# Expert tiles of a decoder kernel: the first product computed transposed, with copied weight chunks as the stationary operand and biases as one value per partition

## Chip, cores and metric

One Trainium2 chip, one of its cores. The metric is the device time of one execution in microseconds; lower is better. A program of this size is one launch with no work on the host.

## The reference

Six pre-norm residual layers act on x of shape 4 × 512 × 128: causal attention with 16 heads (A0), cross attention on 77 context rows (X0), a mixture of experts (M0), attention (A1), single-head cross attention (X1) and a quantized convolutional feed-forward layer (F1). The change lies in M0:

```
logits = xn @ gate_w + gate_b            # 8 experts
weights, indices = top_k(logits, 2); weights = softmax(weights)
h = xn @ w1[e] + b1[e]                   # 128 -> 1024
xh, gh = split(h, 2)                     # "plain" and "gated" half, 512 each
out_e = (silu(gh) * xh) @ w2[e] + b2[e]  # 512 -> 128
x = x + sum over the two chosen experts of weight * out_e
```

## The kernel before

All five engines run long hand-ordered queues. The first stream is A0 and X0 in 32 units (one unit: four heads of one batch), then M0, then a second stream with A1, X1 and F1.

**Loads.** SyncE (SP) issues nearly all DMAs from one queue, in an order written by hand. In unit `g` of the first stream it issues `load_sp` for unit `g + 3` (the stacked queries and keys of four heads go into a slot of `stk`, two DMAs of 256 KB), then `shift_sp` for unit `g + 1` (a small DMA from `negT` into `stk`, L625, one per unit), then two entries of the list `later` (weights and biases of later layers), then one 512 KB piece of the expert weights `w12`. Among the entries of `later` is `b1_gated`, the gated half of M0's first bias, spread over 128 partitions: 2048 KB. The plain half, `b1_plain`, lies in the bytes of `stk` and is loaded by `moe_sp` once X0's scores are done, 2048 KB too. TensorE's `max_pe` of unit `g + 2` runs beside the scores of unit `g` and waits for its slot of `stk`.

**M0.** Every token goes to two experts. GpSimd scatters the normed rows into expert regions of a DRAM tensor, 128 rows a tile; 39 tiles (`BUSY_TILES`) are then worked one after the other, each with the expert number read from a coded register (`codes`, `experts`). Per tile:

- SP loads 128 rows into `x_in` (two buffers), TensorE transposes them (`turn`, L1753), VectorE copies them to `x_inT` and computes the row numbers `y_at` (`turned`, L1637, L1638).
- `hidden` (L1759): for z = 1 (gated) and z = 0 (plain) one fp32 product, `x_inT` stationary, 512 columns of `w1` moving. It appears as two matmul instructions, as does every fp32 product here. The results have tokens on the partitions.
- VectorE adds `b1_gated` (L1644), ScalarE computes Silu (L1802), VectorE adds `b1_plain` (L1651) and multiplies (L1655) into `act`.
- TensorE transposes `act` in four chunks (`turn_act`, L1767), ScalarE copies the result to `actT` (L1806), TensorE computes the second product, four chunks of `actT` stationary, 128 columns of `w2` moving (`output`, L1774: eight instructions), VectorE adds `b2` (L1661), GpSimd stores the rows by an indirect DMA (L1742).

`x_inT`, `silu`, `y_sb` and the two banks for the hidden product (`hid`) are double; `act`, `actT` and `y_bank` are single. TensorE's order for tile t of the loop is: gated product of t + 1, transposes of `act` of t, turn of t + 2, plain product of t + 1, output of t. In the trace `probs` is the memory of `silu`, `y_sb`, `x_in` and `x_inT`; `oT` is `act`, `okT` is `actT`, `w` is the memory of the expert weights.

Of the kernel before, what the change touches and what calls it, by code (L numbers as in the profile page):

```python
# [11 lines left out]
F32 = mybir.dt.float32  # L12
# [239 lines left out]
def build(nc, d, out):  # L252
# [4 lines left out]
    with es:  # L257
# [71 lines left out]
        b1_gated = sb("b1_gated", [P, NE, FF])  # L329
        b1_plain = stk[:].rearrange("p u z h n -> p (u z h n)").bitcast(F32).rearrange("p (e n) -> p e n", e=NE)  # L330
# [1152 lines left out]
        def second_stream_sp(e):  # L1483
# [13 lines left out]
            diff expo plus recip gates zeroed scattered xT xT_out gated_half gated plain_half plain silu act actT actT_out y_in y_out  # L1497
# [86 lines left out]
        def moe_dve(e, ln):  # L1584
# [56 lines left out]
            def gated(t, ex):  # L1641
                k = t % 2
                e.wait_ge(m["gated_half"], t + 1)
                e.tensor_tensor(silu[:, k], hid[k][1], b1_gated[:, bass.ds(ex[t], 1)].rearrange("p o n -> p (o n)"), ALU.add)\  # L1644
                    .then_inc(m["gated"], 1)

            def product(t, ex):
                k = t % 2
                e.wait_ge(m["plain_half"], t + 1)
                wait(e, m["act"], t)  # L1650
                e.tensor_tensor(act[:], hid[k][0], b1_plain[:, bass.ds(ex[t], 1)].rearrange("p o n -> p (o n)"), ALU.add)\  # L1651
                    .then_inc(m["plain"], 1)
# [11 lines left out]
            e.wait_ge(s_biases, 16 * 2)  # L1664
            e.wait_ge(m["tile_e"], CODED + 2)
            code = codes(e)
            ex = experts(code, 0)
            for t in range(2):
                turned(t)
            gated(0, ex)  # L1670
            product(0, ex)
            for t in range(BUSY_TILES):
                if t + 1 < BUSY_TILES:
                    if t + 1 not in ex:
                        ex |= experts(code, t + 1)
                    gated(t + 1, ex)
                if t + 2 < BUSY_TILES:
                    turned(t + 2)
                if t + 1 < BUSY_TILES:
                    product(t + 1, ex)  # L1680
                output(t, ex)
# [24 lines left out]
        act = oT[:, 0]  # L1706
        actT = okT
# [7 lines left out]
        t_bank = bank_st[3]  # L1715
# [29 lines left out]
        def moe_pe(e, ln):  # L1745
# [9 lines left out]
            def hidden(t, ex, z):  # L1755
                if z == 1:
                    e.wait_ge(m["xT_out"], t + 1)
                    wait(e, m["act"], t - 1)
                e.matmul(hid[t % 2][z], x_inT[:, t % 2],  # L1759
                         w1[:, bass.ds(ex[t], 1), z * FF:(z + 1) * FF].rearrange("p o n -> p (o n)"),  # L1760
                         start=True, stop=True).then_inc(m["gated_half" if z else "plain_half"], 1)

            def turn_act(t):
                e.wait_ge(m["act"], t + 1)
                wait(e, m["actT_out"], t)
                for c in range(FC):
                    mm = e.transpose(t_bank[:, c * P:(c + 1) * P], act[:, c * P:(c + 1) * P], ident[:])  # L1767
                mm.then_inc(m["actT"], 1)

            def output(t, ex):  # L1770
                e.wait_ge(m["actT_out"], t + 1)
                e.wait_ge(m["y_out"], FREE + t)
                for c in range(FC):
                    mm = e.matmul(y_bank[:, 0:D], actT[:, c * P:(c + 1) * P],  # L1774
                                  w2[:, bass.ds(ex[t], 1), c, :].rearrange("p o n -> p (o n)"), start=(c == 0), stop=(c == FC - 1))
# [5 lines left out]
            ex = experts(code, 0)  # L1781
            for z in (1, 0):
                hidden(0, ex, z)
            for t in range(BUSY_TILES):
                if t + 1 < BUSY_TILES:
                    if t + 1 not in ex:
                        ex |= experts(code, t + 1)
                    hidden(t + 1, ex, 1)
                turn_act(t)
                if t + 2 < BUSY_TILES:  # L1790
                    turn(t + 2)
                if t + 1 < BUSY_TILES:
                    hidden(t + 1, ex, 0)
                output(t, ex)

        def moe_act(e, ln):
# [3 lines left out]
            def gate_part(t):  # L1800
                e.wait_ge(m["gated"], t + 1)
                e.activation(silu[:, t % 2], silu[:, t % 2], ACT.Silu).then_inc(m["silu"], 1)  # L1802

            def turned_act(t):
                e.wait_ge(m["actT"], t + 1)
                e.copy(actT[:], t_bank).then_inc(m["actT_out"], 1)  # L1806

            gate_part(0)
            for t in range(BUSY_TILES):
                turned_act(t)  # L1810
                if t + 1 < BUSY_TILES:
                    gate_part(t + 1)
# [150 lines left out]
        def weights_pe(e):  # L1963
            e.wait_ge(f["abs"], 2)
# [274 lines left out]
        halves = d["M0_b1"].rearrange("o (e z n) -> o e z n", e=NE, z=2)  # L2239
        later += [(b1_gated[:], halves[:, :, 1].to_broadcast([P, NE, FF]))]  # L2240
# [148 lines left out]
```

## Time and profile before

| what | value |
|---|---|
| three runs | 845.04, 848.81, 851.72 us; median 848.81 us |
| span of the profiled execution | 844.2 us |
| TensorE busy, share of the span | 689.9 us, 82% |
| VectorE busy | 589.3 us, 70% |
| ScalarE busy | 414.1 us, 49% |
| GpSimd busy | 285.0 us, 34% |
| mean granted TensorE clock | 0.880 of full |

The profiled execution has no time of its own beside its span; the fastest timed run lies 0.8 us above that span and the median 4.6 us above it. A busy share is a mean over stages with different limits, so what the change is worth is read stage by stage.

### The profile page before, as it was taken

Reading aid. Unit: us, or ns where it says so; the run is one execution under the profiler, and the core shown is the slowest. Engines: PE = TensorE matmul, PEld = TensorE weight load, DVE = VectorE, ACT = ScalarE, POOL = GpSimd, SP = SyncE. Lnnn points to the kernel's source line nnn. Section 1 sums busy time; section 2 is a strip of 40 time slices with the busy share of each in tenths; the row PEclk is TensorE's granted clock in tenths of the full one; section 3 lists DMA queues with packets and bytes.
Section 4 is the critical chain, followed back from the end, with each engine's and each line's share of the span. In section 5 each row is a group of like instructions: output and inputs, shape, how many; then the busy total and the mean of one; then the engine's idle time right before and its main releaser. Section 6 shows DMA issues by size and latency. Waiting matters only on the chain.

```text
span 844.2 us, 14947 instructions
## 1 busy us (share of the span) xinstructions
PE 689.9 (82%) x4693; PEld 333.1 (39%) x4698; DVE 589.3 (70%) x1606; ACT 414.1 (49%) x708; POOL 285.0 (34%) x504
## 2 busy tenths in 40 slices
PE   2759999989888998239999973668899988999887
PEld 1334454444434445116666641212232322324443
DVE  3757678686646664738788753778889898962664
ACT  1332556555665443003333322137688787885454
POOL 4742454543532233723222320122423133230310
PEclk9875999998988657569999995559999999999998
DMA  7443665482232314311111113521122210000000
GB/s 217 150 176 107 190 183 155 125 262 78 83 93 53 94 47 128 96 36 38 43 41 45 39 29 105 169 75 52 63 90 89 64 52 26 26 2 1 0 26 26
DMA packets 74780, 71.27 MB, mean 84 GB/s; under 512 B 14560, under 2 KB 67168, under 8 KB 74704
## 3 DMA queue, kind: packets, MB, share of 16 engines
q1 hardware_dynamic: 72000, 64.84, 25.1%
q0 software_dynamic: 2272, 4.69, 1.8%
q8 instruction: 40, 0.66, 0.3%
q10 hardware_dynamic: 432, 0.79, 0.3%
q14 instruction: 36, 0.29, 0.1%
HBM read 41.90 MB, written 28.00 MB: 83 GB/s over the span
## 4 chain that ended last, share of the span: by engine, by line
PE 62%; DVE 18%; issue 7%; POOL 4%; DMA 4%; ACT 4%; SPq 1%; DVEq 0%; POOLq 0%; ACTq 0%
PE bank_pv L732 11%; DVE mx L590 9%; PE bank_turn L574 8%; PE bank_scores L2024 5%; PE bank_scores L684 4%; PE bank_scores L1774 4%; PE bank_turn L1759 4%; PE bank_scores L1759 4%; PE bank_turn L751 3%; POOL routed_tokens L1726 2%; PE bank_scores L1767 2%; PE bank_turn L793 2%; PE bank_turn L528 2%; DMA stk<-stack_A 1%; DVE stats L450 1%
## 5 line engine op out<-in xcount | busy, mean ns | idle before, releaser
L590 DVE TENSOR_REDUCE mx<-bank_turn 128x1 f32<-128x512 f32 (+3 forms) x452 | 260.6, 616 | 67.2 <-PE bank_turn L579 35.8
L574 PE MATMUL bank_turn<-stk 64*128 64x77 bf16 (+4 forms) x708 | 164.2, 314 | 29.4 <-DVE mx L590 17.7
L684 PE MATMUL bank_scores<-stk 64*128 64x512 bf16 (+4 forms) x576 | 176.4, 372 | 4.8 <-ACT probs L705 3.6
L709 ACT ACTIVATE probs<-bank_scores 128x1024 f32<-128x1024 f32 (+4 forms) x160 | 117.2, 768 | 111.7 <-PE bank_scores L684 111.4
L705 ACT ACTIVATE probs<-bank_scores 128x512 f32<-128x512 f32 x256 | 138.6, 605 | 35.3 <-PE bank_scores L684 34.3
L732 PE MATMUL bank_pv<-probs,vsl 128*32 128x512 f32 (+4 forms) x1152 | 143.0, 570 | 2.8 <-POOL probs L717 1.9
L574 PEld LDWEIGHTS bank_turn<-stk 64*128 64x128 bf16 x708 | 54.4, 102 | 134.5 <-DVE mx L590 63.2
L717 POOL TENSOR_SCALAR_AFFINE_SELECT probs<-probs 128x256 f32<-128x256 f32 x128 | 52.1, 410 | 78.1 <-ACT probs L709 76.8
L1742 POOL DMA_INDIRECT expert_outputs<-probs,y_at x39 | 37.4, 960 | 101.0 <-DVE probs L1661 98.0
L477 POOL TENSOR_TENSOR rstd<-var,mhalf 128x4 f32<-128x4 f32 x24 | 25.4, 1058 | 119.2 <-DVE var L456 119.1
L1806 ACT COPY okT<-bank_scores 128x512 f32<-128x512 f32 x39 | 22.9, 587 | 80.8 <-PE bank_scores L1767 80.8
L528 PE MATMUL bank_turn<-ident,xn 128*128 128x128 f32 x60 | 13.2, 358 | 57.0 <-DVE xn L471 57.0
L684 PEld LDWEIGHTS bank_scores<-stk 64*128 64x128 bf16 (+1 forms) x576 | 47.6, 97 | 30.0 <-ACT probs L705 18.0
L579 PE MATMUL bank_turn<-behind_even,even_q 64*128 64x128 bf16 x256 | 53.4, 230 | 0.0
L578 PE MATMUL bank_turn<-behind_pair,pair_q 64*128 64x128 bf16 x256 | 53.4, 230 | 0.0
L1774 PEld LDWEIGHTS bank_scores<-w,okT 128*128 128x128 f32 x312 | 37.7, 191 | 25.0 <-issue 25.0
L2024 PE MATMUL bank_scores<-f_w1c,w 128*128 128x512 f32 x96 | 46.0, 616 | 0.4 <-ACT w L537 0.4
L1774 PE MATMUL bank_scores<-w,okT 128*128 x312 | 43.9, 284 | 0.8 <-ACT okT L1806 0.8
L604 POOL CAST neg<-mx 128x16 bf16<-128x16 f32 x33 | 6.5, 198 | 111.5 <-DVE mx L590 98.1
L590 DVE TENSOR_REDUCE mx<-bank_scores 128x1 f32<-128x512 f32 x60 | 40.8, 680 | 3.0 <-PE bank_scores L574 2.9
L1759 PE MATMUL bank_turn<-w,probs 128*128 x80 | 42.5, 616 | 0.0
L542 ACT COPY xnT<-bank_turn 128x512 f32<-128x512 f32 x19 | 11.1, 584 | 56.9 <-PE bank_turn L528 56.9
(299 smaller groups left out, 1179.7 us busy)
## 6 DMA issues: line engine op xcount, KB each, us to landing
stk<-stack_A SPq DMA_DIRECT2D x64, 256.0 KB, 3.2
w<-in_M_w SPq DMA_DIRECT2D x12, 512.0 KB, 4.7
stack_A<-parts SPq DMA_DIRECT2D x15, 384.0 KB, 3.1
stack_A<-fill SPq DMA_DIRECT2D x8, 512.0 KB, 5.1
stk<-stack_X SPq DMA_DIRECT2D x16, 256.0 KB, 2.7
stack_A<-parts SPq DMA_DIRECT2D x15, 256.0 KB, 3.2
probs<-routed_tokens SPq DMA_DIRECT2D x39, 65.0 KB, 1.8
b_gated<-in_M_b SPq DMA_DIRECT2D x1, 2048.0 KB, 11.9
```

What stands on the lines that cost most here:

```text
L574: mm = e.matmul(o, stk[r, slot, 0, pp, qt * P:(qt + 1) * P], stk[r, slot, 1, pp, 0:keys], start=True, stop=not a.causal)
L578: e.matmul(o, half(pair_q, j), half(behind_pair, j), start=False, stop=False)
L579: mm = e.matmul(o, half(even_q, j), half(behind_even, j), start=False, stop=True)
L590: e.tensor_reduce(o.rearrange("p h q -> p q h"), bank_of((g, m))[:, 0:k * keys].rearrange("p (q h k) -> p q h k", q=len(tiles), h=len(hs)) ...
L684: mm = e.matmul(score_bank(g, kt, i)[0:a.kp, 0:S - q0], stk[r, slot, 1, pp, kt * P:kt * P + a.kp], stk[r, slot, 0, pp, q0:S], start=True, ...
L705: e.activation(probs[:, probs_of(g, kt), j + 2 * pp], score_bank(g, kt, i), ACT.Exp, scale=1 / math.sqrt(HD)).then_inc(s["probs"], 1)
L709: e.activation(probs[0:a.kp, probs_of(g, kt), j:HG:2, 0:n], bank_scores[0:a.kp, 2 * j:2 * j + 2, 0:n], ACT.Exp, scale=1 / math.sqrt(HD)).t ...
L717: e.affine_select(out=o, in_=o, compare_op=ALU.is_ge, fill=0.0, base=0, pattern=[[0, 2], [1, P]], channel_multiplier=-1).then_inc(s["maske ...
L732: mm = e.matmul(bank_pv[VW * h:VW * (h + 1), q0:S], vsl[0:a.kp, slot, kt, h, :], probs[0:a.kp, probs_of(g, kt), h, 0:S - q0], start=(kt == ...
L1759: e.matmul(hid[t % 2][z], x_inT[:, t % 2], w1[:, bass.ds(ex[t], 1), z * FF:(z + 1) * FF].rearrange("p o n -> p (o n)"), start=True, stop=T ...
L1774: mm = e.matmul(y_bank[:, 0:D], actT[:, c * P:(c + 1) * P], w2[:, bass.ds(ex[t], 1), c, :].rearrange("p o n -> p (o n)"), start=(c == 0), ...
L2024: e.matmul(bank, f_xT[:, b, j * P + tap:j * P + tap + P], f_w1c[:, tap], start=(tap == 0), stop=False)
```

## The change

The first product of each expert tile is computed transposed: chunks of 128 columns of `w1` are the stationary operand and `x_inT` (128 tokens) moves, so that the result has hidden features on the partitions and tokens along the free axis. It then needs no transpose ahead of the second product: `turn_act`, `turned_act`, `actT` and `t_bank` go away. A bias is now one value per partition: Silu takes it as ScalarE's bias operand, the plain half takes it in one VectorE instruction that adds it and multiplies by Silu's result. The 1024 biases of the eight experts are loaded as 64 rows of 128 values (`b1_rows`, 32 KB), transposed once on TensorE and copied to `b1_cols` by VectorE; `b1_gated` and `b1_plain` and their two DMAs of 2048 KB go away. VectorE's and ScalarE's elementwise work on the hidden layer is now four instructions of 128 × 128 each, with the expert's column read through a register.

```
-        b1_gated = sb("b1_gated", [P, NE, FF])
-        b1_plain = stk[:]... (a view)
+        b1_rows, b1_cols = sb("b1_rows", [NE * 2 * FC, P]), sb("b1_cols", [P, NE, 2 * FC])
+        w_now = sb("w_now", [P, 2, 2 * FF])
...
 # VectorE
-            def gated(t, ex): ...
             def product(t, ex):
                 k = t % 2
                 e.wait_ge(m["plain_half"], t + 1)
-                wait(e, m["act"], t)
-                e.tensor_tensor(act[:], hid[k][0], b1_plain[...ex[t]...], ALU.add).then_inc(m["plain"], 1)
-                e.wait_ge(m["plain"], t + 1)
-                e.wait_ge(m["silu"], t + 1)
-                e.tensor_tensor(act[:], act[:], silu[:, k], ALU.mult).then_inc(m["act"], 1)
+                for c in range(FC):
+                    e.wait_ge(m["silu"], FC * t + c + 1)
+                    e.scalar_tensor_tensor(act[:, k, c * P:(c + 1) * P], hid[k][0][:, c * P:(c + 1) * P],
+                                           b1_cols[:, bass.ds(ex[t], 1), c], silu[:, k, c * P:(c + 1) * P],
+                                           ALU.add, ALU.mult).then_inc(m["act"], 1)
+            def weight(t, ex):
+                e.tensor_copy(w_now[:, t % 2, 0:FF], w1[:, bass.ds(ex[t], 1), 0:FF]...).then_inc(m["plain_w"], 1)
 # prologue: weight(0), weight(1), turned(0), turned(1), product(0), weight(2)
 # loop for t: turned(t + 2), product(t + 1), weight(t + 3), output(t)
...
 # TensorE
+                e.wait_ge(m["gated_w" if z else "plain_w"], t + 1)
                 for c in range(FC):
-                e.matmul(hid[t % 2][z], x_inT[:, t % 2], w1[...512 columns...], start=True, stop=True)
+                    o = z * FF + c * P
+                    mm = e.matmul(hid[t % 2][z][:, c * P:(c + 1) * P], w_now[:, t % 2, o:o + P], x_inT[:, t % 2],
+                                  start=True, stop=True)
-            def turn_act(t): ...
 # loop for t: hidden(t + 1, 1), turn(t + 2), hidden(t + 1, 0), output(t)
...
 # ScalarE, loop for t
+                e.wait_ge(m["gated_half"], t + 1)
+                for c in range(FC):
+                    e.activation(silu[:, t % 2, c * P:(c + 1) * P], hid[t % 2][1][:, c * P:(c + 1) * P], ACT.Silu,
+                                 bias=b1_cols[:, bass.ds(ex[t], 1), FC + c]).then_inc(m["silu"], 1)
+                    weight(t + 2)      # e.copy of the gated half into w_now, after the four
-            turned_act(t), gate_part(t + 1)
...
 # SyncE
-            e.dma_start(b1_plain, halves[:, :, 0].to_broadcast([P, NE, FF])).then_inc(s_biases, 16)
-        later += [(b1_gated[:], halves[:, :, 1].to_broadcast([P, NE, FF]))]
+        later += [(b1_rows[:], d["M0_b1"].rearrange("o (r p) -> (o r) p", p=P))]
...
 # ahead of the loop, in weights_pe and weights_dve
+            e.transpose(b1_bank, b1_rows[:], ident[0:NE * 2 * FC, 0:NE * 2 * FC]).then_inc(m["b1_in"], 1)
+            e.wait_ge(m["b1_in"], 1)
+            e.tensor_copy(b1_cols[:].rearrange("p e c -> p (e c)"), b1_bank).then_inc(m["b1"], 1)
```

## Rows read from the trace of the kernel before

**Rows 1.** Windows: start:end, length, busy us (count) per engine, clock, DMA share, GB/s.

```profile
173.00:186.00 13.00, 11.88 (x143) 5.91 (x140) 11.87 (x36) 7.63 (x13) 5.95 (x15) 1.00 0.95 293
186.00:188.00 2.00, 0.00 (x0) 0.00 (x0) 1.47 (x3) 0.00 (x0) 1.96 (x4) 1.00 1.07 391
190.00:197.00 7.00, 7.00 (x43) 3.16 (x44) 2.75 (x7) 4.13 (x6) 1.64 (x4) 0.54 0.44 154
...
381.00:500.00 119.00, 118.33 (x622) 72.81 (x620) 95.37 (x220) 42.83 (x74) 35.52 (x37) 1.00 0.15 41
```

**Rows 2.** Chain that ended last, one expert tile: start, us, what.

```profile
430.51 0.96 PE bank_scores L1774 x8
431.47 0.86 PE bank_turn L1759 x2
432.33 0.44 PE bank_scores L1767 x4
432.77 0.11 PE bank_turn L1753
...
433.74 0.96 PE bank_scores L1774 x8
```

**Rows 3.** Timeline around the first tiles and the last: start, us, engine, line, idle before.

```profile
352.91 1.28 ACT L1802 ACT_TABLE_LOAD   x1
...
370.61 0.45 PE L1753 MATMUL bank_turn<-ident,probs 128*128 128x128 f32 x1 [14.31 <-DMA probs<-routed_tokens]
...
376.85 0.66 PE L1767 MATMUL bank_scores<-ident,oT 128*128 128x128 f32 x4 [0.75 <-DVE oT L1655]
...
501.41 1.15 PE L1774 MATMUL bank_scores<-w,okT 128*128 x8 [0.78 <-ACT okT L1806]
```

**Rows 4.** Chain that ended last, the first four matmuls of the loop.

```profile
371.98 3.28 PE bank_turn L1759 x4
```

**Rows 5.** Instructions of line 1686, VectorE's queue: durations, first and last start.

```profile
L1686 DVEq TENSOR_LOAD <-tile_e x10: 297/302/557, 359.8 to 365.6; - x10
```

**Rows 6.** Timeline in X0's end: eight weight loads for eight 8-column products.

```profile
335.87 0.97 PEld L1508 LDWEIGHTS bank_turn<-gate_w,xnT 128*128 128x128 f32 x8
```

**Rows 7.** Groups by line: count | busy us, mean ns | idle before.

```profile
L1806 ACT COPY okT<-bank_scores 128x512 f32<-128x512 f32 x39 | 22.9, 587 | 80.8 <-PE bank_scores L1767 80.8
...
L1638 DVE SCALAR_TENSOR_TENSOR y_at<-probs,tile_f 128x1 uint32<-128x1 f32 x39 | 8.2, 210 | 0.0
...
L2079 DVE SCALAR_TENSOR_TENSOR x_sb<-bank_turn,f_hback,x_sb 128x128 f32<-128x128 f32 x8 | 2.8, 349 | 9.3 <-PE bank_turn L2072 9.3
...
L1984 DVE TENSOR_SCALAR f_w<-f_w,f_mean 128x512 f32<-128x512 f32 x1 | 0.5, 487 | 0.0
...
L1661 DVE TENSOR_TENSOR probs<-bank_scores,rest 128x128 f32<-128x128 f32 x37 | 10.5, 283 | 0.0
```

**Rows 8.** Timeline of ScalarE in A1: four 128 × 128 activations with an operand per partition.

```profile
673.38 1.14 ACT L1951 ACTIVATE w<-bank_scores,x_rec 128x128 f32<-128x128 f32 x4 [1.11 <-PE bank_scores L1942]
```

**Rows 9.** Timeline of SyncE's queue and of TensorE in A0.

```profile
138.93 0.53 SPq L625 DMA_DIRECT2D stk<-negT  x1
...
159.60 0.53 SPq L625 DMA_DIRECT2D stk<-negT  x1
...
173.82 0.57 SPq L1173 DMA_DIRECT2D b_gated<-in_M_b  x1
...
180.40 0.53 SPq L625 DMA_DIRECT2D stk<-negT  x1
...
188.52 0.23 PE L574 MATMUL bank_turn<-stk 64*128 64x128 bf16 x1 [2.74 <-DMA stk<-stack_A]
...
205.84 0.53 SPq L625 DMA_DIRECT2D stk<-negT  x1
```

**Rows 10.** Chain that ended last, a piece in A0.

```profile
176.17 12.31 DMA stk<-stack_A
```

**Rows 11.** DMA issues: form, count, KB each, median us to landing.

```profile
stk<-stack_A SPq DMA_DIRECT2D x64, 256.0 KB, 3.2
...
b_gated<-in_M_b SPq DMA_DIRECT2D x1, 2048.0 KB, 11.9
```

More of the change, by code:

```diff
@@ L1496, in build @@
             place placed zero_at zeros tokens floor cum tile_le tile_held tile_f tile_at tile_row tile_e y_at
-            diff expo plus recip gates zeroed scattered xT xT_out gated_half gated plain_half plain silu act actT actT_out y_in y_out
+            diff expo plus recip gates zeroed scattered xT xT_out b1_in b1 gated_w plain_w gated_half plain_half silu act y_in y_out
             weighed""".split()}
@@ L1649, in product @@
                 e.wait_ge(m["plain_half"], t + 1)
[L1650 to L1655 removed]
+                for c in range(FC):
[4 more added lines that the diff above has]
+            def weight(t, ex):
+                e.tensor_copy(w_now[:, t % 2, 0:FF], w1[:, bass.ds(ex[t], 1), 0:FF].rearrange("p o n -> p (o n)"))\
+                    .then_inc(m["plain_w"], 1)
             def output(t, ex):
@@ L1667, in moe_dve @@
             ex = experts(code, 0)
+            e.wait_ge(s_experts, 16 * W_PIECES)
+            for t in range(2):
+                weight(t, ex)
             for t in range(2):
                 turned(t)
-            gated(0, ex)
             product(0, ex)
+            weight(2, ex)
             for t in range(BUSY_TILES):
[L1673 to L1676, printed above, removed]
                 if t + 2 < BUSY_TILES:
@@ L1680, in moe_dve @@
                     product(t + 1, ex)
+                if t + 3 < BUSY_TILES:
+                    if t + 3 not in ex:
+                        ex |= experts(code, t + 3)
+                    weight(t + 3, ex)
                 output(t, ex)
@@ L1780, in moe_pe @@
                 turn(t)
-            ex = experts(code, 0)
             for z in (1, 0):
-                hidden(0, ex, z)
+                hidden(0, z)
             for t in range(BUSY_TILES):
+                if t % CODED == 0:
+                    ex = experts(code, t)
                 if t + 1 < BUSY_TILES:
[L1786 to L1789, printed above, removed]
+                    hidden(t + 1, 1)
                 if t + 2 < BUSY_TILES:
@@ L1792, in moe_pe @@
                 if t + 1 < BUSY_TILES:
-                    hidden(t + 1, ex, 0)
+                    hidden(t + 1, 0)
                 output(t, ex)
@@ L1798, in moe_act, with weight @@
             e.activation(gate_t[:, 1], gate_t[:, 0], ACT.Exp).then_inc(m["expo"], 1)
[L1800 to L1808, printed above, removed]
-            for t in range(BUSY_TILES):
-                turned_act(t)
-                if t + 1 < BUSY_TILES:
-                    gate_part(t + 1)
+            e.wait_ge(m["tile_e"], CODED + 2)
+            code = codes(e)
+            e.wait_ge(m["b1"], 1)
+            def weight(t):
+                e.copy(w_now[:, t % 2, FF:], w1[:, bass.ds(ex[t], 1), FF:].rearrange("p o n -> p (o n)"))\
+                    .then_inc(m["gated_w"], 1)
+            e.wait_ge(s_experts, 16 * W_PIECES)
+            ex = experts(code, 0)
+            for t in range(2):
+                weight(t)
+            for t in range(BUSY_TILES):
+                e.wait_ge(m["gated_half"], t + 1)
+                for c in range(FC):
+                    e.activation(silu[:, t % 2, c * P:(c + 1) * P], hid[t % 2][1][:, c * P:(c + 1) * P], ACT.Silu,
+                                 bias=b1_cols[:, bass.ds(ex[t], 1), FC + c]).then_inc(m["silu"], 1)
+                if t + 2 < BUSY_TILES:
+                    if t + 2 not in ex:
+                        ex |= experts(code, t + 2)
+                    weight(t + 2)
         def moe_sp(e):
             e.wait_ge(s["scores"], exps_at(2 * UN))
-            e.dma_start(b1_plain, halves[:, :, 0].to_broadcast([P, NE, FF])).then_inc(s_biases, 16)
             e.dma_start(b2, d["M0_b2"].rearrange("o (e d) -> o e d", e=NE).to_broadcast([P, NE, D])).then_inc(s_biases, 16)
```

31 lines of the change are left out of this document (8 added, 23 removed).

## Prediction

> **What bounds the kernel now.** The change touches two places that lie far apart, so I read two stages. For the expert loop I took the table of windows first. Between 381 and 500 us TensorE is busy 118.3 of 119 us at full clock, VectorE 95.4, ScalarE 42.8 and GpSimd 35.5, and the DMA engines have a share of 0.15 [rows 1]. The reader is to see that one engine fills this stage and that no other comes near. The chain of waits says the same: a tile is nothing but TensorE pieces, 0.96 for the second product, 0.86 for the gated product, 0.44 for the four transposes of the activation, 0.11 for the turn of a coming tile, and 0.86 again for the plain product (that piece repeats the one before it), 3.23 us from one second product to the next [rows 2]. Work that the other engines gain or lose counts only where it starts to make TensorE wait.
>
> The second place is the load of `b1_gated`, which runs 200 us ahead of the experts, in A0. There I went the other way round: the chain of waits has one DMA piece of 12.31 us, a load of stacked queries and keys [rows 10], where the list of DMA issues has 3.2 us as the median of the same kind [rows 11]. SyncE's queue shows what was issued just ahead of it: `b_gated`, 2048 KB [rows 9, 11]. The window from 173 to 186 us has the DMA engines at 0.95 and 293 GB/s; in the two microseconds after it TensorE does nothing [rows 1], and it starts again at 188.52 us with the load named as what it waited for [rows 9]. After that pause the granted clock is at its lower level, 1.2 GHz: 0.54 on average from 190 to 197 us [rows 1].
>
> **The change part by part.** *TensorE per tile.* Removed: the four transposes, 0.44. Changed: each 512-column product of two instructions, 0.86, becomes four products of 128 columns, eight instructions with a weight load each. The nearest row is the second product, which has exactly this form, fp32, 128 × 128 held, 128 columns moving, eight instructions: 0.96 [rows 2]. So each half grows by 0.10. The new tile is 3 × 0.96 + 0.11 = 2.99 us, 0.24 less than 3.23. Is a run of 24 such pairs as fast as a run of eight that stands behind a long product? The bound from the other side is a run in which the moving side is only 8 columns wide, so that the weight loads alone set the pace: eight in 0.97 us [rows 6], 0.121 each. The two agree, so the run should be limited by loads at 0.121, which makes 24 × 0.121 + 0.11 = 3.01. I take 2.99 and keep 3.02 as the end of the range for the tile.
>
> *The loop.* Before, it runs from 371.98 us [rows 4] to the end of the last second product, 501.41 + 1.15 = 502.56 [rows 3], 130.6 us. 39 × 3.23 is 126.0. Of the other 4.6, the cold start is 3.28 − 1.72 = 1.56 (the first two products at half clock) [rows 4, 2], 0.75 is a wait for the first activation and 0.78 one for the last copy [rows 3]. After: 39 × 2.99 = 116.6, the same cold start, 1.6, and about 0.9 at the end, where the last two second products still share one bank, whose result VectorE has to take in between (0.28 [rows 7] and the hand-overs). The wait of 0.75 should go: ahead of the first second product TensorE now has both products of tile 1 and a turn to do, 2.03 us even at full clock, where before it had one. Sum 119.1, a gain of 11.5 us. Bounds: 39 × 3.02 and all of the old 4.6 kept give 122.4, a gain of 8.2; 2.97 per tile and 2 us around it give 12.8.
>
> *VectorE per tile.* Four add-and-multiply instructions from PSUM with a per-partition operand, 0.349 each by the row of that form and size [rows 7], 1.40; a 128 × 512 copy between SBUF tiles, by the nearest row of that shape with one tensor operand 0.487 [rows 7]; the copy of the turned rows, which I price like the 128 × 128 addition at 0.283, `y_at` 0.210, and the output 0.283 [rows 7]. Sum 2.66, below 2.99, and near the 95.37 / 119 × 3.23 = 2.59 that it has per tile now [rows 1]. The sum counts full durations, though successive instructions overlap, so it is an upper end except for register work. The order matters more: `weight` stands ahead of `output`, and `product` ahead of both. If the plain product ends at time 0, `product` ends by 1.5 and `weight` by 2.0, `output`, for which TensorE is ready at 0.96, by 2.3, and the bank is wanted again at 2.99. The turned rows come at 0.96 + 0.96 + 0.11 = 2.03 and are out at about 2.8, wanted at 3.95. `product` itself is wanted only by the next second product, at 2.99. TensorE waits for none of these. Without that cover the bank would be the first to be late: every further 0.7 us on VectorE ahead of `output` would show up in full.
>
> *ScalarE per tile.* Four 128 × 128 activations take 1.14 us in a row of that form [rows 8], the copy of the gated half 0.587, priced as the copy of that size out of PSUM [rows 7]; the removed copy cost the same. Sum 1.73. The gated product ends 1.07 us ahead of time 0, so Silu is done at about 0.1, behind the point where `product` could start by at most that. The copy for tile t + 3 is due four microseconds later. *GpSimd and the loads* keep their places; a tile period of 2.99 leaves both double-buffered chains nearly six microseconds, so nothing there.
>
> *Ahead of the loop.* Added: one transpose and one small copy for the biases, VectorE's and ScalarE's first weight copies, and ScalarE's own ten register loads. TensorE waits 14.31 us for the first tile's rows [rows 3], and that wait ends at 370.6. VectorE reads its codes until 366 [rows 5] and then has two copies of 0.49 to do, done at 367.5. ScalarE had its work done since its table load at 352.9 [rows 3]. All is hidden; without cover it would cost 0.2 (biases) and 1.0 (copies). One thing may move: the table load of 1.28 us for Silu [rows 3] may now come after the wait for the first gated product. Then Silu of tile 0 ends 2.4 us after that product; TensorE still has its three other products and a turn, over 3 us. Nothing.
>
> *The load of `b1_gated`.* It becomes 32 KB. At 293 GB/s [rows 1] 2048 KB are 7.0 us, so the load for the next unit, issued at 176.2 and landed at 188.5 [rows 10], would land at 181.5. TensorE had work until 185.8 (188.52 − 2.74 [rows 9]), so 4 us of margin. What is the pause worth? Not only its 2.74 us, because the half clock behind it stretches the work. The per-unit DMA of L625 gives a yardstick: two units take 159.60 − 138.93 = 20.67 us, and the two units in the same places of the next batch take 205.84 − 180.40 = 25.44 [rows 9]. The difference is 4.8 us, and this is what I take. Lower end 2.7 (the pause alone) or zero (see the rivals), upper end 6. *The load of `b1_plain`* runs when SyncE has no load for TensorE in its queue and GpSimd's scatter sets the pace; I take nothing, between 0 and a gain of 1.
>
> *Sum.* Against the profiled span: 844.2 − 11.5 − 4.8 = 827.9. The median of the three runs lies 4.6 us above the span, so the median after is 832.5.
>
> A rule to weigh here: the Trainium skill, "TensorE: Matmul & The Clock Gate", section "The mechanism", says that a weight load overlaps a running matmul only when the two use different row groups. Every load of this loop uses all rows. By that rule a pair would take the load and the product one after the other. The trace of this kernel speaks against it (eight pairs in 0.96 us [rows 2] are as fast as eight loads alone [rows 6]). I give it the rival below.
>
> **The rivals.** *A: the pause in A0 gives nothing back.* Either the next load of `stk`, behind `f_taps` and an expert piece, is late instead, or VectorE, busy 1.47 of those 2 us [rows 1], ends the interval. Against it: the margin of 4 us. It leaves 844.2 − 11.5 + 4.6 = 837.3.
>
> *B: the 24 pairs don't keep the pace.* TensorE's queue has eight semaphore waits a tile, as before, but only thin instructions between them. If they cost 0.2 us a tile, the loop gains 3.7 and the time is 840.3. For it: TensorE's lead over the waits is shorter in instructions of 0.12 us. Against it: the transposes and the turn, 0.11 each with waits between them, leave no gap [rows 2].
>
> *C: weight loads are no longer hidden.* Each pair takes 0.121 (load) and a quarter of 0.43 (product), 0.228; a tile takes 24 × 0.228 + 0.11 = 5.6 us, 39 × 2.35 = 92 us more than before, so 936. This is what the rule above would do here. The eight pairs in 0.96 [rows 2] speak against it.
>
> *D: VectorE becomes the bound, slower than before.* Each of the four steps of `product` waits for its own semaphore and reads its bias address through a register. From 0.08 us of extra time for each step VectorE passes TensorE (2.66 + 4 × 0.08), and from 0.14 on a tile is slower than before; with A0's gain the whole kernel is slower from 0.18. Were each step as long as two instructions, 0.349 + 0.283, a tile would take 3.79, the loop 22 us more, and the time would be 848.8 + 22 − 4.8 = 866. Against it: VectorE's instructions in this loop already use registers and 20% of its time is free [rows 1].
>
> **How the numbers follow.** Forecast 832.5: 0.66. A, 837.3: 0.17. B, 840 to 844: 0.07. C: 0.02. D: 0.04. What I don't see: 0.04. A measurement of this kernel can't tell a change of under about 1%, 8.5 us, from none. Forecast and A and some of B and of the unseen lie below 840.3: faster 0.87. Same: 0.07. Slower: C, D and a bit, 0.06. The range: the forecast's own bounds, 8.2 and 2.7 for the small gain (837.9) and 12.8, 6 and 1 for the large one (829.0), A's 837.3 with the small loop gain (840.6), and the scatter of the three runs, −3.8 and +2.9 around the median, about half of which I add. I take 826 to 842.
>
> **What would show it.** In the chain of the loop pieces of 0.96, 0.11, 0.96, 0.96 and a period of 2.99; TensorE busy in the whole stage; no idle time of TensorE with VectorE or ScalarE as the releaser beyond the first and last tile. In A0 no DMA piece of over 5 us near 176, no pause of TensorE at 186, full clock there, and an interval of L625 of about 20.7 us for the two units. The prediction would be wrong if the period were over 3.1, if VectorE had no idle time in the loop, or if another load of `stk` took the place of the late one.

## The result and the profile after

The kernel after the change takes 822.62 us (median of four runs, 819.51 to 826.33), the kernel before 848.07 us beside it (four runs, 845.04 to 851.72): ratio 0.9711, 95% interval 0.9665 to 0.9757. Faster, as forecast, but 3.4 us below the low end of the range (826). Ratios and their intervals leave out, here and below, the runs that took over 1.5% more than the fastest of their kernel. A second series of the same kernel (e5_after_again, below) gave a ratio of 0.9778 (0.9744 to 0.9812), so the first one lies at the good end of the scatter. Where the gain comes from is read stage by stage. The head of the page of after:

```profile
span 817.7 us, 16027 instructions
PE 668.6 (82%) x5006; PEld 363.9 (45%) x5011; DVE 568.3 (70%) x1685; ACT 432.6 (53%) x825; POOL 283.4 (35%) x504
PEclk9875999999988766659999965579999999999999
```

To divide the 26.5 us between the two spans (844.2 and 817.7) I used events that both traces have: the 28 rows of L625 in the first stream, the first turn of M0 and the end of the last second product. A0 and X0 in the table are these stretches, not the whole layers.

| stretch | before | after | gain |
|---|---|---|---|
| start to first L625 | 67.29 | 65.20 | 2.1 |
| A0: 1st to 14th L625 | 138.55 | 133.74 | 4.8 |
| X0: 14th to 28th L625 | 94.09 | 95.55 | −1.5 |
| to the first turn of M0 | 70.68 | 69.26 | 1.4 |
| expert loop, with the two first turns | 131.95 | 113.20 | 18.8 |
| rest | 341.64 | 340.75 | 0.9 |

The loop holds 18.8 of it, and 11.5 were forecast there. How far can the rows be trusted? There are twelve profiles, these two and one for each experiment below, and over all of them the first L625 falls at 64.65 to 67.29 us and the stretch from the 28th to the first turn takes 68.80 to 71.62, in no order that follows the kernels. The gains of 2.1 and 1.4 lie inside that scatter, and so does the −1.5 of X0, which takes 94.1 to 101.5. Two rows stand out of it: A0, 137.8 to 139.2 with the large load in it and 133.7 to 135.4 without, and the loop, 131.95 to 132.57 in the four profiles of the old form and 113.16 to 113.42 in the four of the new one. Its chain of waits, one tile of after, beside [rows 2]:

```profile
425.67 0.89 PE bank_scores L1761 x8
426.56 0.89 PE bank_scores L1769 x8
427.46 0.89 PE bank_turn L1761 x8
428.35 0.11 PE bank_turn L1752
428.46 0.89 PE bank_turn L1761 x8
429.35 0.89 PE bank_scores L1769 x8
```

From one second product (L1769) to the next are 429.35 − 426.56 = 2.79 us, where it was 3.23. Every piece is TensorE's, as before, and each group of eight takes 0.89, which is 0.1116 for one instruction with its weight load. Windows of after, for [rows 1] (columns as there):

```profile
173.00:186.00 13.00, 11.45 (x141) 5.93 (x136) 12.05 (x35) 6.99 (x12) 7.48 (x18) 1.00 0.71 220
186.00:188.00 2.00, 2.00 (x26) 1.19 (x25) 1.59 (x5) 2.00 (x4) 1.18 (x4) 1.00 0.08 29
190.00:197.00 7.00, 6.67 (x69) 3.45 (x68) 4.98 (x10) 3.22 (x7) 2.27 (x7) 1.00 0.46 142
381.00:470.00 89.00, 89.00 (x800) 89.00 (x799) 66.30 (x256) 52.79 (x160) 30.64 (x32) 1.00 0.18 49
```

In the last line TensorE and its weight loads are both busy in all 89 us, 800 matmuls at 89 / 800 = 0.111 each; 32 tiles went through. VectorE has 66.30 / 32 = 2.07 us of work per tile, ScalarE 1.65. In the first three lines the pause of two microseconds at 186 is gone and the clock at 190 to 197 is 1.00 (0.54 before). Waits of after in the same 89 us (engine, line, releaser: us in total, times, longest):

```profile
POOL expert_outputs L1741 <- DVE y_at L1638: 58.6, 32, 2.1
ACT probs L1808 <- PE bank_scores L1761: 18.3, 16, 1.1
DVE oT L1646 <- ACT probs L1808: 18.1, 31, 0.6
```

VectorE waits 0.58 us a tile for Silu, ScalarE 1.1 for TensorE, and no line has TensorE waiting for either. Timeline around the first tiles and the last, beside [rows 3, 4]:

```profile
363.75 0.45 PE L1752 MATMUL bank_turn<-ident,probs 128*128 128x128 f32 x1 [13.70 <-DMA probs<-routed_tokens]
...
364.94 3.62 PE L1761 MATMUL bank_turn<-probs,w_now 128*128 128x128 f32 x16
366.98 1.28 ACT L1808 ACT_TABLE_LOAD   x1 [11.88 <-PE bank_turn L1761]
...
475.80 1.15 PE L1769 MATMUL bank_scores<-w,oT 128*128 x8 [1.03 <-DVE probs L1658]
```

The table load for Silu did move behind the wait for the first gated product, and TensorE has no idle time behind it: it was still at work on the other 24 instructions and the turn. The wait of 0.75 in tile 0 is gone, and at the end there is one of 1.03. SyncE's queue of after, for [rows 9]:

```profile
171.72 0.59 SPq L1173 DMA_DIRECT2D b_rows<-in_M_b  x1
178.28 0.58 SPq L625 DMA_DIRECT2D stk<-negT  x1
...
198.94 0.54 SPq L625 DMA_DIRECT2D stk<-negT  x1
```

The two units take 198.94 − 178.28 = 20.66 us, where they took 25.44, and 20.67 was forecast.

### The profile page after: what moved, and what is told of

It is laid out like the page before. It is cut to its first block, busy times and chain, and to the rows that moved or that the text cites. A ratio compares the mean times of both kernels' runs of the same rounds, so it can differ in the third digit from the quotient of the medians.

```text
span 817.7 us, 16027 instructions
## 1 busy us (share of the span) xinstructions
PE 668.6 (82%) x5006; PEld 363.9 (45%) x5011; DVE 568.3 (70%) x1685; ACT 432.6 (53%) x825; POOL 283.4 (35%) x504
## 4 chain that ended last, share of the span: by engine, by line
PE 61%; DVE 19%; issue 7%; POOL 5%; ACT 4%; DMA 3%; SPq 1%; DVEq 0%; ACTq 0%; POOLq 0%
PE bank_pv L732 11%; DVE mx L590 10%; PE bank_turn L574 8%; PE bank_scores L2027 5%; PE bank_turn L1761 4%; PE bank_scores L684 4%; PE bank_scores L1761 4%; PE bank_scores L1769 4%; PE bank_turn L751 3%; POOL routed_tokens L1725 2%; PE bank_turn L793 2%; DVE stats L450 2%; PE bank_turn L528 2%; DVE xn L471 2%; PE bank_turn L578 1%
## 5 line engine op out<-in xcount | busy, mean ns | idle before, releaser
L1761 PE MATMUL bank_turn<-probs,w_now 128*128 128x128 f32 x320 | 42.6, 283 | 0.0
L1769 PE MATMUL bank_scores<-w,oT 128*128 x312 | 41.3, 276 | 1.0 <-DVE probs L1658 1.0
L1761 PEld LDWEIGHTS bank_turn<-probs,w_now 128*128 128x128 f32 x320 | 40.4, 199 | 0.0
L1761 PE MATMUL bank_scores<-probs,w_now 128*128 128x128 f32 x304 | 39.5, 277 | 0.0
```

The costliest lines, as they stand in the source:

```text
L1761: mm = e.matmul(hid[t % 2][z][:, c * P:(c + 1) * P], w_now[:, t % 2, o:o + P], x_inT[:, t % 2], start=True, stop=True)
L1769: mm = e.matmul(y_bank[:, 0:D], act[:, t % 2, c * P:(c + 1) * P], w2[:, bass.ds(ex[t], 1), c, :].rearrange("p o n -> p (o n)"), start=(c = ...
```

## Experiments

Two questions were open: why an eight-instruction group takes 0.89 and not 0.96, and whether the 4.8 us of A0 reach the end. Kernels measured in one series share their runs of the kernel before. Of the edits only the lines that matter are shown; `...` marks what is left out.

**The large load, back in its place.** In after, the list `later` gets a 2048 KB load again, at the old place, and the small load of `b1_rows` goes behind `f_taps`. Nothing reads what the large one brings.

```
+        spare = sb("spare", [P, NE, FF])        # w_now lies in it
...
+        later += [(spare[:], halves[:, :, 1].to_broadcast([P, NE, FF]))]
+        later += [(f_taps[:, k], d["F1_taps"][k:k + 1, :].to_broadcast([P, FF])) for k in range(3)]
         later += [(b1_rows[:], d["M0_b1"].rearrange("o (r p) -> (o r) p", p=P))]
-        later += [(f_taps[:, k], d["F1_taps"][k:k + 1, :].to_broadcast([P, FF])) for k in range(3)]
```

> The changed kernel, with the load of the gated half of the first bias (2048 KB) back at its old place in SyncE's queue, into memory that nothing reads; the computation is complete. Theory 1 (the load delays the next load of stk and TensorE pauses): about 4.8 us over the changed kernel, 827.5, with a pause of TensorE of 2 to 3 us near 184 us, a load of stk of 10 us or more, half clock behind it, and 25.4 us for the two units that take 20.7 without it. Rival (the pause had another cause, or differs from run to run): within 1.5 us of the changed kernel's 822.6, two units 20.7.

Ratio 0.9776 (0.9718 to 0.9835), median 830.45 us. TensorE's timeline has the pause again:

```profile
186.86 0.23 PE L575 MATMUL bank_turn<-stk 64*128 64x128 bf16 x1 [2.33 <-DMA stk<-stack_A]
```

The two units take 23.28 us instead of 20.66, A0 137.78 instead of 133.74. So the load does make the pause. The 25.4 expected for the two units didn't come: behind this pause the clock from 190 to 197 us was 0.94, where before it was 0.54, so what a pause costs isn't always the same. In the time of the kernel the load can't be found. After was not run in this series, and its two own series give opposite answers: against the first (0.9711) the kernel with the load is worse by 0.0065, 5.5 us, against e5_after_again (0.9778) by nothing.

**The large load moved, in the kernel before.** `b1_gated` is loaded by `moe_sp`, next to `b1_plain`.

```
-            e.wait_ge(s_biases, 16 * 2)
+            e.wait_ge(s_biases, 16 * 3)             # VectorE
...
-        later += [(b1_gated[:], halves[:, :, 1].to_broadcast([P, NE, FF]))]
+            e.dma_start(b1_gated[:], halves[:, :, 1].to_broadcast([P, NE, FF])).then_inc(s_biases, 16)   # moe_sp
```

> The kernel before, its computation complete; only the load of b1_gated is moved, from A0 to the end of X0, where b1_plain is loaded. Theory 1: 4.8 us faster than before, 843.3, two units 20.7 us in A0, and no cost at its new place, since the bias is first read 45 us later. Rival: the load costs as much where it goes, by delaying GpSimd's scatter or the zero rows: 848.

Twelve runs: 847.34 us, ratio 1.0009 (0.9974 to 1.0045). The trace has the two units at 20.67 and A0 at 134.32 us, 4.2 less than before, and the late load costs nothing that shows (68.80 us to the first turn, before 70.68). Still the kernel isn't faster; the interval leaves room for a gain of at most 0.26%, 2.2 us. In this trace X0 takes 100.39 us instead of 94.09.

**The kernel before once more**, unchanged, for a second profile of it.

> The kernel before once more, unchanged, to see how far two traces of one kernel differ outside the places of the change: the first us of A0 (2.1 us between the two traces), the way from X0 to the first tile. If the 2.1 us at the start are scatter of the first loads, the first L625 should fall anywhere between 65 and 68 us; if they belong to the change, it should be at 67.3 again, and at 65.2 in all kernels without the bias loads.

It took 852.34 us. The first L625 is at 66.41 us here, between the 67.29 of before and the 65.20 of after; with e5_after_again at 67.05, the 2.1 us at the start don't belong to the change. In X0 this profile of the same kernel differs from the first one. Window of X0, the first profile of before:

```profile
210.00:305.00 95.00, 85.24 (x732) 42.06 (x728) 58.18 (x211) 53.12 (x75) 31.02 (x68) 0.82 0.27 76
```

and the second one:

```profile
210.00:305.00 95.00, 88.00 (x688) 41.99 (x687) 55.67 (x202) 51.16 (x71) 30.56 (x67) 0.74 0.27 75
```

The granted clock is 0.74 of full instead of 0.82, fewer matmuls fit into the same 95 us, and X0 takes 99.70 us instead of 94.09. This swing of 5.6 us is as large as what A0 gives, and it isn't caused by the change. The 94.09 of the table above is a good X0, and no evidence on the load. The two units of A0 take 24.40 us here, not 25.44.

**The copy in two halves, in the kernel before.** The first two chunks of the second product (four instructions) wait for the first half of `actT` only.

```
-                e.wait_ge(m["actT_out"], t + 1)      # TensorE, output
+                    if c % 2 == 0:
+                        e.wait_ge(m["actT_out"], 2 * t + c // 2 + 1)
...
-                e.copy(actT[:], t_bank).then_inc(m["actT_out"], 1)
+                for h in range(2):
+                    e.copy(actT[:, h * 2 * P:(h + 1) * 2 * P], t_bank[:, h * 2 * P:(h + 1) * 2 * P]).then_inc(m["actT_out"], 1)
```

> The kernel before, with ScalarE's copy of the transposed activation in two halves, each with its own signal; the computation is complete. Theory 2 (the 0.96 us of the second product before hold a wait of 0.07 us for this copy; a pair of weight load and 128-column product takes 0.112 anyway): the piece of the second product goes to 0.89, the tile from 3.23 to 3.16, the kernel 2.7 us faster, 845.3. Rival (the 0.96 belong to this form of product behind 512-column ones): 0.96, 3.23, 848.1.

Ratio 1.0004 (0.9965 to 1.0043). Its chain, one tile:

```profile
427.37 0.86 PE bank_scores L1759 x2
428.23 0.89 PE bank_scores L1775 x8
429.12 0.86 PE bank_turn L1759 x2
429.99 0.51 PE bank_scores L1767 x4
430.50 0.11 PE bank_turn L1753
```

The second product takes 0.89 here, in the old kernel, once its operand is early: 0.07 of the 0.96 was a wait for ScalarE's copy. The transposes take 0.51 instead of 0.44, so the 0.07 came back as a wait for `act`. The traces show why it is just this much: from the end of the plain product to the first weight load of the transposes are 1.60 us before (430.51 to 432.11) and 1.61 here (428.23 to 429.84), with VectorE's addition and multiplication, 0.69 each, in them. TensorE comes 0.07 earlier, its operand doesn't. So the tile of before hung on ScalarE and VectorE at once, and mending one place gave nothing. The timeline of before has the place (VectorE and ScalarE rows left out but one):

```profile
429.57 0.59 ACT L1806 COPY okT<-bank_scores 128x512 f32<-128x512 f32 x1 [2.11 <-PE bank_scores L1767]
...
430.31 0.86 PEld L1774 LDWEIGHTS bank_scores<-w,okT 128*128 128x128 f32 x7 [0.63 <-issue]
```

The first weight load of the second product starts at 430.31, 0.15 after the copy's end at 430.16, and stood 0.63 idle before that. "Issue" hid a wait.

**After once more**, with **both large loads back in after** beside it (their bytes unread; the second one where `moe_sp` had it).

> The changed kernel once more, unchanged, for more runs beside those of the same chip and for a second trace. Theory: the median falls within 1% of 822.6; its runs spread over 7 us or more with the mean granted clock, as those of the kernel before do (842 at 0.883, 851 at 0.865), since X0's units run at full or half clock from one run to the next. Rival (the spread belonged to the pause in A0 alone): under 3 us between the lowest and the highest.

> The changed kernel with both loads of 2048 KB back at their old places, into memory that nothing reads; the computation is complete. So only the expert loop differs from the kernel before. Theory (the loop alone gives 0.44 us a tile and 1.6 at its ends): 18.8 us faster than before, 828; the loop is 111.8 us long and a tile 2.79. Rival (part of the loop's gain comes from the missing loads): a tile over 2.8. The load of the plain half should cost nothing beyond the first one's 5 to 8 us over the changed kernel; if it delays GpSimd's scatter, up to 2.5 more.

826.19 us (ratio 0.9778, 0.9744 to 0.9812) and 827.44 us (0.9789, 0.9745 to 0.9832). The six runs of after lie 5.1 us apart, between the two expectations for their spread. The loop takes 113.30 and 113.42 us, the two units of A0 20.66 and 25.39. With both loads the change keeps 846.52 − 827.44 = 19.1 of 846.52 − 826.19 = 20.3 us, which is what the loop gives by the traces. What the loads add, about 1 us, isn't told from zero, nor from 4.8 by this pair alone (0.0011, give or take 0.0055).

**No transposes, in the kernel before.** The four transposes and ScalarE's copy are left out; `act` goes untransposed into the second product, and the output addition reads a constant instead of the product. `act` has two buffers here, as in after. This prices the removed part.

```
-                turn_act(t)                          # TensorE
...
-                turned_act(t)                        # ScalarE
...
-                    mm = e.matmul(y_bank[:, 0:D], actT[:, c * P:(c + 1) * P],
+                    mm = e.matmul(y_bank[:, 0:D], act[:, t % 2, c * P:(c + 1) * P],
```

> The kernel before with the four transposes of the activation and ScalarE's copy left out: the second product reads act as it stands (two buffers), which is another result, and VectorE's output adds a constant to the bias instead of the product. Theory (the change gains by the missing transposes and loses 0.03 us for each half that is held in chunks): a tile of 3.23 - 0.44 - 0.07 = 2.72, 0.07 below the changed kernel's 2.79, 39 x 0.51 = 20 us faster than before, 827. Rival (the chain over VectorE, which tied with TensorE in the run with the copy in halves, sets a tile): 2.75 to 3.0, and waits of TensorE for VectorE.

827.21 us, ratio 0.9759 (0.9702 to 0.9816), loop 111.22 us, 20.7 less than before. Chain, one tile, and the window of the loop:

```profile
428.13 0.89 PE bank_scores L1766 x8
429.02 0.86 PE bank_scores L1758 x2
429.88 0.11 PE bank_turn L1752
429.99 0.86 PE bank_scores L1758 x2
430.85 0.89 PE bank_scores L1766 x8
```

```profile
381.00:461.00 80.00, 80.00 (x381) 50.20 (x380) 73.82 (x177) 18.31 (x29) 26.76 (x29) 1.00 0.18 48
```

The tile is 2.72: the transposes were worth 3.23 − 2.72 = 0.51 (0.44 of their own and the 0.07). The change then pays 2.79 − 2.72 = 0.07 for its four times as many, four times as thin instructions: two halves at 0.893 − 0.86 = 0.03 each. VectorE has 73.82 of 80 us of work in this kernel, so a form that only got rid of the transposes would stand close to its limit; in after VectorE has 59.41 of 80.

**Half the moving columns, in after.** The first product takes 64 of the 128 tokens (the others aren't computed, and the output addition reads a constant), with the same weight loads.

```
-                    mm = e.matmul(hid[t % 2][z][:, c * P:(c + 1) * P], w_now[:, t % 2, o:o + P], x_inT[:, t % 2],
+                    mm = e.matmul(hid[t % 2][z][:, c * P:c * P + 64], w_now[:, t % 2, o:o + P], x_inT[:, t % 2, 0:64],
```

> The changed kernel with only 64 of the 128 tokens moving in the chunks of the first product, so half of each tile isn't computed, and VectorE's output adds a constant to the bias instead of the product. What sets the 0.112 us of a pair? If the weight load does: the pieces of the first product stay at 0.89 and a tile at 2.79. If the product does (0.107 for 128 columns at full clock by the 0.43 of 512): the pieces fall towards 0.45 and a tile towards 1.9 to 2.3, where VectorE's or ScalarE's work would be next.

One run, 824.57 us. The chain:

```profile
427.98 0.95 PE bank_scores L1769 x8
428.92 0.84 PE bank_scores L1761 x8
429.76 0.12 PE bank_turn L1752
429.88 0.84 PE bank_scores L1761 x8
430.72 0.95 PE bank_scores L1769 x8
```

A piece of the chain ends with its last product, so the thin group (0.84) hands 0.06 to the group behind it (0.95); what counts is the period, 430.72 − 427.98 = 2.74 us, 0.05 less than in after. Sixteen of the 25 instructions move half the columns, and the tile gets 2% shorter. The weight load, or something as long that comes once per instruction, sets the pace; the moving side adds 0.05 / 16 = 0.003 us to each of them at most. Whatever it is goes by TensorE's clock: at the loop's start, where the granted clock is 0.50, sixteen of these instructions take 3.32 us, 0.21 each. The loop as a whole is no shorter than in after (113.51 us against 113.20), because here the granted clock rose from 0.50 to 1.00 only at 376.6 us, 8.4 us behind the start of the first product, and in after at 369.1, 4.0 us behind it. That costs this kernel 2.2 us more at its start, about as much as the shorter tiles give.

**How much room VectorE has.** In after, one more 128 × 512 copy per tile stands ahead of `weight` in VectorE's queue; in the second kernel two, the second of which waits for the first. Nothing reads what they write.

```
+                if t > 1:
+                    wait(e, m["spare0"], t - 2)
+                    e.tensor_copy(spare[:], w1[:, bass.ds(ex[t], 1), 0:FF].rearrange("p o n -> p (o n)")).then_inc(m["spare0"], 1)
```

> The kernel after, with one more 128 x 512 copy per tile in VectorE's queue, directly ahead of the weight copy (it reads the plain half of w1 and writes a tile that nobody reads). Theory (TensorE's 24 pairs and the turn set the period, VectorE is far from it): VectorE has 66.30 / 32 = 2.07 us of work per tile in the windows of after, a copy takes 0.42, so 2.49 of 2.79; the tile stays 2.79 and the loop near 113.2 us. Rival (VectorE is nearly the bound because of its order and its waits: what is put ahead of the output is late for the one bank of the second product): the tile grows by up to 0.42 us to 3.21, the loop by up to 16 us.

> As the run before, with two more copies per tile, the second waiting for the first. Theory: 2.07 + 0.84 = 2.91 us of work per tile plus one hand-over between the two copies (0.03 to 0.1 us) is over 2.79, so VectorE becomes the bound; a tile takes 2.95 to 3.05 us, the loop 6 to 10 us more than 113.2, and the kernel has 818 to 834 us. Rival (VectorE's room is smaller than busy time says, waits for TensorE and ScalarE in its fixed order come on top): a tile takes 3.3 us or more, the loop 20 us more, and the whole gain of the loop is gone. Second rival (busy time overstates VectorE, successive instructions overlap): 2.79 unchanged.

828.62 us (ratio 0.9762, 0.9659 to 0.9866) and 838.21 us (0.9821, 0.9683 to 0.9958); 818 to 834 had been expected for the second. The loop takes 115.21 us with one copy, 2.0 more than after, or 0.05 per tile; with two it takes 124.23, 11.0 more, 0.28 per tile, a period of 3.07. Window, waits and single instructions with two copies:

```profile
381.00:470.00 89.00, 84.77 (x719) 81.71 (x719) 80.58 (x291) 47.84 (x145) 27.52 (x29) 1.00 0.17 44
```

```profile
PEld bank_scores L1775 <- issue: 7.0, 15, 0.9
DVE oT L1647 <- ACT probs L1814: 6.4, 14, 0.6
PE bank_scores L1775 <- DVE probs L1664: 0.7, 1, 0.7
```

```profile
382.96 1.15 PE L1775 MATMUL bank_scores<-w,oT 128*128 x8 [0.74 <-DVE probs L1664]
...
474.49 0.28 DVE L1664 TENSOR_TENSOR probs<-bank_scores,rest 128x128 f32<-128x128 f32 x1
...
475.22 0.97 PEld L1775 LDWEIGHTS bank_scores<-w,oT 128*128 128x128 f32 x8 [0.31 <-issue]
```

Now the weight loads have idle time, 7.3 of 89 us, nearly all ahead of the second product. It waits for `act` and for its one bank. `act` is not the late one: VectorE's last write to it ends 1.7 to 2.0 us ahead of these weight loads. What ends last is the addition of `b2` (L1664), which frees the bank; it is named as the releaser at 382.96, and it ends 0.35 to 0.6 us ahead of each such load (474.77 to 475.22 in the lines above). That is the time of the hand-over itself: the last tile of after, where TensorE does nothing but wait for this addition, has 475.35 to 475.80, 0.45. In after the addition ends 0.71 us ahead of the next second product, so only 0.71 − 0.45 = 0.26 us were free there. The theory gave 2.95 to 3.05; it is a little more. VectorE is busy 80.58 of the 89 us and waits 6.4 for Silu, 98% together, so its queue, with ScalarE's Silu in it, sets the period. The rival of 3.3 and more doesn't hold. VectorE had 0.42 us per tile to spare almost for nothing, not 0.84.

## Why the prediction was right and wrong

*What bounds the loop:* right for after, and nearly right for before. Every piece of both chains is TensorE's, and e9 and e10 show how far VectorE is from it in after. In before the distance was nothing: 0.07 of the 0.96 was a wait for ScalarE, and e3 shows that TensorE couldn't have been 0.07 faster without waiting for VectorE. "No other comes near", read from 95.4 us busy of 119, was too much.

*TensorE per tile:* this is the step that failed, as a mis-sized term. "Each half grows by 0.10. The new tile is 3 × 0.96 + 0.11 = 2.99", with 0.121 per weight load as the bound from the other side. Measured: 3 × 0.893 + 0.11 = 2.79. A half grows by 0.03, and the second product shrinks by 0.07. Two rows seemed to agree, and both held something else. The 0.96 of [rows 2] had a wait for ScalarE's copy in it (e3: 0.89 as soon as the copy is early). The 0.97 of [rows 6] runs from the first load's start to the last one's end, and one load alone lasts 0.19 in after (`LDWEIGHTS ... x1` in the timeline) though the next starts 0.11 later: 7 × 0.111 + 0.19 = 0.97. The prediction had a better row in its own hands, the four transposes in 0.44 [rows 2], four weight loads with 128 columns each at 0.11.

*The loop:* 111.8 us (365.15, the start of the first product by the chain, to 475.80 + 1.15 = 476.95) instead of 119.1. The period accounts for 39 × (2.99 − 2.79) = 7.8 of the 7.3; the other −0.5 is the rest, 3.0 instead of 2.5: the last wait is 1.03 instead of 0.9, and the cold start 1.95 instead of 1.6 (the first 24 instructions take 3.42 + 1.21 us by the chain, and 2.68 at full clock). Of the old 4.6 the prediction named only 3.1 and let the other 1.5 go without a reason; since 3.0 came, this did no harm.

*VectorE and ScalarE:* neither makes TensorE wait, as said, but for the last tile. VectorE's 2.66 was an upper end indeed (busy 2.07: the four steps of `product` take 1.12 and not 1.40, the copy 0.42 and not 0.49); ScalarE's 1.73 was 1.65. Rival D, up to 0.28 us more per step, is out: a step takes 0.344 us, as its row said. The warning about work ahead of `output` was right in the place: in e10 the bank is what comes late. It was wrong in the size of the cover: the 0.7 us leave out the hand-over of 0.45 from VectorE's addition to TensorE's next product, and 0.26 were left. So a copy of 0.42 cost 0.05 already, and two, 0.84, cost 0.28.

*Ahead of the loop:* hidden, the table load too.

*The load of `b1_gated`:* the mechanism in A0 was right, and e1 shows it from the other side. In all six profiles with the load in its old place TensorE pauses for a load of `stk` near 187 us (1.9 to 3.2 us), in none of the six without. That the size was right to 0.1 us is luck: the two units take 20.66 or 20.67 in all six without the load, but 23.28 to 25.70 in the six with it, 24.7 on average, so that the load costs 4.0 there and not 4.8. What failed is taking all of it into the sum: 4.8 us shorter is A0, not the kernel. e2 bounds its worth at 2.2 us; e6 has its best value near nothing, with a wider interval, and e1 can't tell. Rival A foresaw this ("the pause in A0 gives nothing back") for another reason, as no other load is late. Where it goes is not settled. Over the twelve profiles A0 and X0 together take 235.4 us on average in the six with the load in its old place (232.6 to 238.9) and 232.7 in the six without it (229.3 to 235.8). The means differ by 2.7 us, with a swing of 6 us from run to run in each group: part may be given back in X0, part may be there and be lost in the scatter. The mean granted clock of every run says a little more. As an estimate, with one straight line of time over clock for both kernels (490 to 505 us per unit of clock, that is 5 us for 0.01), e2 lies 1.6 us below before at the same clock (standard error 0.4, 12 and 20 runs), and e5 2.6 us below e6 (0.6, six and six). But the kernels without the load in A0 had the lower mean clock, 0.869 against 0.875 and 0.872 against 0.876. So about 2 us look real, about the pause alone, and the half clock saved behind it seems to come back elsewhere. The clock differs by 0.005 to 0.008 from run to run, so this second part isn't shown.

*Rivals B and C:* 24 pairs in a row keep the pace of eight. The Trainium skill, "TensorE: Matmul & The Clock Gate", section "The mechanism", says in its list of what overlaps that a weight load overlaps a matmul only where their row groups differ. The opening of that section of the Trainium skill also lets a load into a background weight buffer go ahead of running matmuls; no trace here shows which buffer a load goes to. The measurement decides against the rule of that list for these loads of all 128 rows: with it a tile would take 5.6 us, and it takes 2.79, TensorE and its loads busy at once in 89 of 89 us.

*The sum and the range:* with the loop's 18.8 in the place of 11.5 the sum of the prediction gives 844.2 − 18.8 − 4.8 + 4.6 = 825.2, and 830.0 if A0 gives nothing. The ten timed runs of after have a median of 824.8 us. As differences, which don't hang on how fast the kernel before was in a series, the two sums are gains of 23.6 and 18.8 us; measured were 25.5 in the first series and 20.3 in the second. Runs that spread over 10 us don't decide between the two. The forecast's two errors pulled opposite ways: the loop was 7.3 too small, and the 4.8 of A0 probably too large for the whole kernel, which would hide part of the first. The range failed by the same term: its low end was built on 2.97 per tile, and 2.79 takes 7.0 us more off; the 822.6 measured would then lie inside.

## What to carry to other kernels

Take the pace of a pipelined instruction from start to start, or from a long run of them divided by its count; the length of a short group holds one instruction's own latency, and perhaps a wait that the trace doesn't name. Where an engine is full, ask whether each of its pieces has its clean length before you price a new one by it, and check this with a second row of another size (4 in 0.44 against 8 in 0.96). When you work out how long an engine may be late, put in the hand-over from one engine to the next, from a place in the trace where nothing else stands between them. A microsecond won in one stage counts only if what follows keeps it: compare two profiles of the same kernel stage by stage before you add up a difference of 5 us in one.

## What the runs showed of the hardware

- fp32 128 × 128 weights with 128 columns moving go at 0.1116 us for each instruction at full clock, 24 in a row with no gap; with half the columns in 16 of 25 the mean is 2.74 / 25 = 0.110. At half clock sixteen of them take 3.42 us, 0.21 each. A 512-column instruction takes 0.43, so four thin instructions (0.446) cost only 4% more.
- The granted clock of the same kernel differs from run to run: before ran 842 us at a mean of 0.883 and 854 at 0.864, after 819.5 at 0.882 and 829.5 at 0.867. In the traces it is mostly X0, with 94 to 101 us. At the start of the loop the clock rose 4.0 us behind the start of the first product in after, and 8.4 us behind it in e8, where half the columns move.
- In the six profiles with it in A0, a 2048 KB load of broadcast rows takes 10.9 to 12.3 us, and a 256 KB load issued just behind it 11.5 to 12.8 instead of 3.2.
- From the end of VectorE's last write to the TensorE work that waited for it the traces have 0.45 us ahead of the second product (475.35 to 475.80 in after) and 0.05 ahead of a weight load of the transposes (432.06 to 432.11 in before). Why the first is so long isn't shown.
